# Local attention: one row of heads over all jobs, ordered by a table of times

## The chip, the cores and the metric

One core of one Trainium2 chip runs the whole program. The metric is the device time of one execution in microseconds (us). The kernel before was run three times: 4954.37, 4963.61 and 4968.31 us, median 4963.61 us. One more execution was profiled: 4963.8 us, its span on the engines 4961.9 us.

The five engines run separate instruction streams, each strictly in its own order, and meet at semaphores: PE (TensorE, matrix products and transposes into the accumulator banks), DVE (VectorE), ACT (ScalarE), POOL (GpSimd) and SP (SyncE, which issues all the DMA transfers here).

## The reference, cut to what matters

A residual stream `x` of 4 batch entries x 256 tokens x 256 features passes six stages: cross attention, convolved attention, a local transformer, cross attention, gated linear attention and a mixture of experts. Only the third stage is touched. It computes, six times (layers):

```python
x = attn_layer(shift_tokens(x), Wqkv[i], q_scale[i], k_scale[i], Wo[i]) + x
x = ffn_layer(shift_tokens(x), ln_g[i], ln_b[i], W1[i], b1[i], W2[i], b2[i]) + x
```

`shift_tokens` takes the second half of the features from the token before. `attn_layer` has 16 heads of 64; queries and keys are normalised per head, scaled and rotated, and each token attends to itself and the 64 before it, with a softmax. `ffn_layer` is a layer norm, a product to 2 x 682 columns, GELU gating and a product back to 256. All is float32. Batch entries do not mix, so layer l of entry b needs only layer l-1 of entry b.

## The kernel before, in words

The stage is the class `Local`. Its unit is a job, one layer of one batch entry: 24 jobs, j = 4 l + b. A job has three parts:

- front: `features` (PE transposes 256 tokens of x and of the shifted rows `xs`, ACT copies them to `xt`); eight `proj` (a 128x512 product for tile 0/1, query/key, half 0/1; DVE multiplies it in three instructions with the rotation tables, ACT squares it, POOL adds the two rotated parts); `sumsq` and `norm` (DVE sums the squares; POOL raises them to the power -1/2, L1577); `scale_k` (DVE scales the keys by their norms); eight `turn` (PE transposes queries or keys, ACT copies them out: two instructions for queries, one for keys); four `values` (product on PE, copy on ACT).
- back: the 16 heads of attention, class `Attention`. A head n passes PE `front` (mask, L965, and scores, L967), DVE maximum and scale, ACT exponential (L1036), then `divide` on DVE and POOL (L1023), PE `turn` of the weights (L976), ACT copy (L1043), and for every second head PE `apply` (weights times values, L987) and an ACT copy into `ot` (L1474). `steps` lays this out: head n's front goes with head n-1's divide and head n-3's turn. Called per job, it ends each job with four steps that have no front. Then two `wo`, the output product (L1853).
- gated: `fs` (three DMAs fetch the rows of x and the shifted rows into `fs`, and cannot start before both `wo` results are added to x), `f_stats`, `f_scale`, `ft` (layer norm and its transposes), six `w1` (L1869) with three `gate` (ACT GELU and a DVE product per chunk; GELU and exponential need different tables on ACT, ACT_TABLE_LOAD), two `w2` (L1879), whose results DVE adds to x.

The DMA step `shift` fetches the shifted rows `xs` for the same batch entry of the next layer: one DMA of 127 partitions (L1538) and one of a single row (L1539). It waits on SP for the end of that entry's second `w2`. `fs` has the same pair of DMAs (L1549, L1550) behind one of all 128 partitions (L1548).

`order()` writes one list, `plan`, and every engine walks that list and does its share of each step. So the list fixes the order on each engine, and all timing follows from the order and the waits. Round n of `order()` runs front of job n, back of job n-1 and gated of job n-2; `even` deals their steps out over 24 ticks.

Products and transposes outside attention share three accumulator banks (5, 6, 7) in turn: use number n takes bank 5 + n % 3 and PE waits until use n-3 has been taken out (`freed`). Scores have two banks: head n's front waits for the exponentials of head n-2. Head 0 of a job waits until all eight `turn` results of its job are copied out. `values` of job j overwrites the values of job j-2, so ACT waits for those `apply` steps (`pv_done`, L1628).

Of the kernel before, what the change touches and what calls it, by code (L numbers as in the profile page):

```python
# [1297 lines left out]
class Local(Stage):  # L1298
# [4 lines left out]
    scale = None  # L1303

# [49 lines left out]
    def order(self):  # L1354
# [13 lines left out]
        for n in range(len(jobs) + 2):  # L1368
            parts = [(part(*jobs[n - lag]), steps, late) for lag, (part, steps, late) in
                     enumerate(((self.front, 24, 0), (self.back, 23, 0), (self.gated, 17, 0.1)))  # L1370
                     if 0 <= n - lag < len(jobs)]
            even(*parts)

    def front(self, l, b):
        put = self.plan.append
        if b == 2 and l + 1 < DEPTH:
            put(("load_front", l + 1))
        if b == 3 and l + 1 < DEPTH:
            put(("tables", l + 1))
        yield ()  # L1380

        def project(tile, sec):
            for half in range(2):
                put(("proj", l, b, tile, sec, half))
                yield ()
                put(("sumsq", l, b, tile, sec, half))
            put(("norm", l, b, tile, sec))

        def turn(tile, sec):
            for half in range(2):  # L1390
                put(("turn", l, b, tile, sec, half))
                yield ()

        def values(tile):
            for half in range(2):
                put(("values", l, b, tile, half))
                yield ()
        yield from project(0, 0)
        yield from round_robin(project(0, 1), values(0))
        yield from turn(0, 0)  # L1400
        put(("scale_k", l, b, 0))
        yield from round_robin(project(1, 0), turn(0, 1))
        yield from project(1, 1)
        yield from round_robin(turn(1, 0), values(1))
        if b == B - 1 and l + 1 < DEPTH:
            put(("load_values", l + 1))
        put(("scale_k", l, b, 1))
        yield ()
        if (l, b) != (DEPTH - 1, B - 1):
            l2, b2 = divmod(self.job(l, b) + 1, B)  # L1410
            put(("features", l2, b2))
            if l2 == 0 and b2 + 2 < B:
                put(("shift", 0, b2 + 2))
        yield from turn(1, 1)

    def back(self, l, b):
        put, j = self.plan.append, self.job(l, b)
        for steps in self.at.steps(H * j, [(j, h) for h in range(H)]):
            for s in steps:
                put(("attend", s))  # L1420
# [1177 lines left out]
```

## Time and profile before

| what | value |
|---|---|
| median of three runs | 4963.61 us (4954.37 to 4968.31) |
| profiled execution: time, span | 4963.8 us, 4961.9 us |
| busy PE, DVE, ACT, POOL over the span | 4427.0, 3249.4, 2896.0, 1872.0 us |
| first and last `features` copy of the stage (L1603) | 1361.3 and 3053.7 us after the span's start |
| mean granted PE clock over the span | 0.967 |

The stage runs from about 1360 to 3227 us. "Busy" of PE is modelled: its records overlap, so the length of a PE step is best read from one start to the next. A bracket at the end of a timeline row is the idle time of the engine before it and what ended it; "issue" means that the profile shows nothing that it waited for.

### The profile page before, as it was taken

The page shows a single profiled execution, that of the slowest core. Times are in us where ns is not written, and L with a number is a line of the kernel's source. Part 1 is how long each engine was busy: PE and PEld are TensorE (multiplying, and loading weights), DVE is VectorE, ACT ScalarE, POOL GpSimd, SP SyncE. Part 2 cuts the span into 40 slices and gives each one's busy share as a digit, 9 for nine tenths or more (in the row PEclk, how much of TensorE's full clock was granted, in tenths as well). Part 3 has the DMA queues.
Part 4 walks back from the last instruction along what each step waited for, and adds up shares of the span by engine and source line. Part 5 has one row for each costly group of instructions (what it writes and reads, how often), then busy time and mean ns, then how long its engine had stood idle before and what let it go on. Part 6 is the DMA issues. An engine that isn't in the chain of part 4 may idle for free. (4 is left out here: it accounts for less than half of the span.)

```text
span 4961.9 us, 85570 instructions
## 1 busy us (share of the span) xinstructions
PE 4427.0 (89%) x31624; PEld 3025.6 (61%) x31624; DVE 3249.4 (65%) x7542; ACT 2896.0 (58%) x5798; POOL 1872.0 (38%) x1876
## 2 busy tenths in 40 slices
PE   5899998989789999999999999859999999669999
PEld 3555555547556666666676666635555555358888
DVE  5677777767565666656656666356777777575555
ACT  2666666668556666666666666426666666523332
POOL 2223222215564545445545444223222222035554
PEclk8999999989899999999999999979999999879999
DMA  5655555500110010100001000056555555011110
GB/s 138 131 103 104 104 113 102 94 24 1 56 39 6 23 45 13 54 15 26 33 14 53 16 32 6 13 126 129 108 103 104 110 109 90 12 53 49 49 48 19
DMA packets 189931, 305.60 MB, mean 62 GB/s; under 512 B 19736, under 2 KB 109752, under 8 KB 187832
## 3 DMA queue, kind: packets, MB, share of 16 engines
q1 hardware_dynamic: 189520, 300.13, 27.3%
q8 instruction: 256, 4.19, 0.4%
q14 instruction: 155, 1.27, 0.1%
HBM read 215.81 MB, written 73.40 MB: 58 GB/s over the span
## 5 line engine op out<-in xcount | busy, mean ns | idle before, releaser
L707 DVE TENSOR_REDUCE xa_m_part<-xa_ring 128x1 f32<-128x512 f32 x2048 | 1319.1, 686 | 506.3 <-PE xa_ring L856 491.0
L633 ACT ACTIVATE xa_ex<-xa_sc 128x1024 f32<-128x1024 f32 x1024 | 991.6, 1022 | 114.2 <-PE xa_sc L844 99.0
L856 PE MATMUL xa_ring<-xa_ks,xa_q_base 48*128 48x512 f32 x2048 | 517.8, 498 | 185.6 <-DVE xa_m_part L707 129.4
L870 PE MATMUL xa_pv<-xa_ex,xa_vs 128*17 128x256 f32 x8192 | 547.8, 385 | 1.3 <-issue 1.3
L856 PEld LDWEIGHTS xa_ring<-xa_ks,xa_q_base 48*128 48x128 f32 x2048 | 201.4, 185 | 517.2 <-DVE xa_m_part L707 432.9
L1036 ACT ACTIVATE lt_p<-lt_bank,lt_stat,lt_rq 128x128 f32<-128x128 f32 (+1 forms) x768 | 365.6, 482 | 215.4 <-DVE lt_stat L1006 210.1
L1570 POOL TENSOR_TENSOR lt_r_qk<-lt_r_qk,lt_t_rot 128x512 f32<-128x512 f32 x192 | 243.2, 1267 | 611.1 <-DVE lt_t_rot L1686 606.1
L844 PE MATMUL xa_sc<-xa_q_base,xa_ks 50*128 50x256 f32 x4096 | 423.0, 302 | 26.4 <-ACT xa_k L605 5.2
L844 PEld LDWEIGHTS xa_sc<-xa_q_base,xa_ks 50*128 50x128 f32 x4096 | 346.8, 187 | 117.5 <-ACT xa_vs L620 24.1
L1023 POOL TENSOR_SCALAR lt_p<-lt_p,lt_stat 128x192 f32<-128x192 f32 x384 | 335.0, 876 | 197.8 <-DVE lt_stat L1013 197.8
L2412 PE MATMUL moe_bank<-moe_xp,moe_wp 128*128 128x512 f32 x1536 | 373.3, 392 | 5.9 <-POOL moe_wp L2240 4.2
L1809 PE MATMUL lt_bank<-lt_wqk,lt_xt 128*128 128x512 f32 x768 | 365.5, 599 | 0.7 <-ACT lt_xt L1603 0.7
L555 POOL CAST xa_kp<-xa_k 128x512 fp32r<-128x512 f32 (+1 forms) x144 | 84.4, 586 | 655.7 <-ACT xa_k L613 314.2
L1577 POOL TENSOR_TENSOR lt_nrm<-lt_nrm,minus_half 128x16 f32<-128x16 f32 x96 | 280.5, 2922 | 122.4 <-DVE lt_nrm L1703 121.2
L2412 PEld LDWEIGHTS moe_bank<-moe_xp,moe_wp 128*128 128x128 f32 x1536 | 281.5, 189 | 59.9 <-issue 4.3
L870 PEld LDWEIGHTS xa_pv<-xa_ex,xa_vs 128*17 128x17 f32 x8192 | 188.7, 97 | 198.6 <-issue 59.6
L2275 ACT ACTIVATE moe_sg<-moe_bank 128x512 f32<-128x512 f32 x128 | 76.5, 598 | 341.1 <-PE moe_bank L2412 341.1
L1610 ACT ACTIVATE lt_t_sq<-lt_bank 128x512 f32<-128x512 f32 x192 | 114.6, 597 | 267.3 <-DVE lt_t_rot L1686 267.3
L1869 PE MATMUL lt_bank<-lt_ft,lt_w 128*128 128x256 f32 x1152 | 262.5, 381 | 1.2 <-DVE lt_ft L1751 1.2
L2246 POOL TENSOR_TENSOR moe_hp<-moe_hh,moe_hp 128x512 fp32r<-128x512 f32 x128 | 166.1, 1297 | 256.7 <-ACT moe_hp L2253 256.7
L976 PE MATMUL lt_bank<-ident,lt_p 128*128 128x128 f32 x1152 | 199.3, 282 | 54.7 <-issue 54.7
L1002 DVE TENSOR_REDUCE lt_stat<-lt_bank 128x1 f32<-128x128 f32 (+1 forms) x768 | 210.5, 315 | 44.2 <-PE lt_bank L967 44.0
(281 smaller groups left out, 8755.1 us busy)
## 6 DMA issues: line engine op xcount, KB each, us to landing
xa_ks<-keys SPq DMA_DIRECT2D x384, 256.0 KB, 9.1
keys<-xa_kp SPq DMA_DIRECT2D x128, 512.0 KB, 3.8
xa_cx<-in_ctx_t SPq DMA_DIRECT2D x64, 512.0 KB, 4.9
lt_wqk<-in_lt_wqkv SPq DMA_DIRECT2D x6, 2048.0 KB, 8.4
lt_w<-in_lt_w SPq DMA_DIRECT2D x6, 1536.0 KB, 6.2
xa_q_base<-xa_m_rows SPq DMA_DIRECT2D x512, 2.0 KB
moe_w<-in_moe_wg SPq DMA_DIRECT2D x64, 128.0 KB, 2.2
moe_w<-in_moe_wu SPq DMA_DIRECT2D x64, 128.0 KB, 2.3
```

What stands on the lines that cost most here:

```text
L633: act.activation(x.ex[:, n % x.NE, :, :], x.sc[n % 2][:, :, :], ACT.Exp).then_inc(*x.ex_done.one())
L707: dve.tensor_reduce(x.m_part[:, i % 2, qt, h, ch:ch + 1], x.bank(n + odd), AX.X, ALU.max).then_inc(*x.dve_out.one())
L844: mm = pe.matmul(x.sc[n % 2][:, 2 * odd + pair, :], x.ks[unit % x.NU][rows, 2 * (g % 2) + pair, kt * P:(kt + 1) * P], x.q_base[rows, 2 * g ...
L856: pe.matmul(x.bank(n + odd), x.q_base[rows, pair, b * S + qt * P:b * S + (qt + 1) * P], x.ks[unit % x.NU][rows, pair % 4, ch * 512:(ch + 1 ...
L870: mm = pe.matmul(x.pv[32 * j:32 * j + x.VW, :], x.vs[:, i % x.NV, kt, 4 * g + j, :], x.ex[:, n % x.NE, 2 * (j % 2) + j // 2, :], start=(kt ...
L1023: pool.tensor_scalar(sv, sv, self.stat[:, n % 5, 3, 1:2], None, ALU.mult).then_inc(*self.div_pool.one())
L1036: act.activation(self.p[:, n % 5, to], s[:, at], ACT.Exp, bias=t3[:, 1, q:q + 1], scale=st.scale_of(b, h, slice(q, q + 1)) if st.scale is ...
L1570: pool.tensor_tensor(out, out, self.t_rot[:, t, :], ALU.add).then_inc(*self.rot_add.one())
L1577: pool.tensor_tensor(n[:, 2, :], n[:, 1, :], c.minus_half[:, 0:H], ALU.pow).then_inc(*self.rnorm.one())
L1809: mm = pe.matmul(bank[:, :], self.xt[:, par, k, tile * P:(tile + 1) * P], self.wqk[:, l % 2, k, col:col + 512], start=(k == 0), stop=(k == ...
L1869: mm = pe.matmul(bank[:, gate * S:(gate + 1) * S], self.w1[:, k, gate * FFP + m * P:gate * FFP + (m + 1) * P], self.ft[:, k, :], start=(k ...
L2412: mm = pe.matmul(self.banks[2 * (n % 2) + j][:, :], self.wp[:, wpart, i, j, k * FI:(k + 1) * FI], self.xp[:, xpart, k, at], start=(m == 0) ...
```

## The change: what it does

`order()` no longer runs rounds. Every step of a job has a fixed time, in ticks, from a table; job j adds 24 j; all steps are sorted by time. The heads of all 24 jobs form one row: one call of `steps` over 384 heads, head i at 24.14 + 1.5 i ticks, so the steps without a front come only once, at the very end. Loads, `features` and `shift` have times of their own. The set of steps is the same. In a job's own ticks: first projection at -3.79, last `turn` of keys at 22.93, heads from 24.14 on, `wo` at 56.11 and 56.30, `fs` at 56.72 and `f_stats` at 64.74, `w1` from 69.70 to 74.85, `w2` at 77.48 and 83.33, `shift` at 82.7; `features` of the next job at 15.17. Since job j+1's features come at 15.17 of job j, the job four on, which needs the shifted rows, has its features at 87.17. The order of the head also asks for the change at L1628: half 0 of `values` waits only for the first 8 heads of job j-2, half 1 for all 16.

```diff
--- before.py
+++ after.py
@@ -1301,6 +1301,23 @@
 
     HP = H // 2
     scale = None
+    TICKS, HEADS, FEATURES, SHIFT = 24, 24.14, 15.17, 82.7
+    LOADS = ((16.58, "load_front", 2, ()), (22.82, "tables", 2, ()), (10.8, "load_values", 3, ()),
+             (62.88, "load_back", 3, (0,)), (76.94, "load_back", 3, (1,)), (86.28, "load_back", 3, (2,)))
+    TABLE = ((-3.79, "proj", 0, 0, 0), (-2.03, "sumsq", 0, 0, 0), (-0.97, "proj", 0, 0, 1),
+             (2.44, "values", 0, 0), (2.99, "sumsq", 0, 0, 1), (3, "norm", 0, 0), (3.5, "proj", 0, 1, 0),
+             (3.96, "turn", 0, 0, 0), (4.12, "proj", 0, 1, 1), (5.04, "sumsq", 0, 1, 0),
+             (5.38, "turn", 0, 0, 1), (5.61, "sumsq", 0, 1, 1), (6.7, "values", 0, 1), (6.91, "norm", 0, 1),
+             (7.05, "proj", 1, 0, 0), (8.34, "scale_k", 0), (10.18, "proj", 1, 0, 1), (11.1, "turn", 0, 1, 0),
+             (12.82, "turn", 0, 1, 1), (12.82, "sumsq", 1, 0, 0), (13.07, "sumsq", 1, 0, 1),
+             (13.12, "norm", 1, 0), (13.57, "proj", 1, 1, 0), (13.71, "turn", 1, 0, 0),
+             (13.71, "proj", 1, 1, 1), (14.98, "values", 1, 0), (15.57, "sumsq", 1, 1, 0),
+             (15.59, "sumsq", 1, 1, 1), (17.36, "turn", 1, 0, 1), (19.45, "norm", 1, 1),
+             (20.84, "values", 1, 1), (21.54, "scale_k", 1), (21.93, "turn", 1, 1, 0),
+             (22.93, "turn", 1, 1, 1), (56.11, "wo", 0), (56.3, "wo", 1), (56.72, "fs"), (64.74, "f_stats"),
+             (66.43, "f_scale"), (68.92, "ft"), (69.7, "w1", 0), (69.75, "w1", 1), (69.83, "gate", 0),
+             (71.18, "w1", 2), (72.3, "w1", 3), (72.49, "gate", 2), (74.21, "w1", 4), (74.85, "w1", 5),
+             (74.86, "gate", 4), (77.48, "w2", 0), (83.33, "w2", 1))
 
     def __init__(self, c, g):
         super().__init__(c)
@@ -1365,93 +1382,24 @@
         put(("features", 0, 0))
         put(("shift", 0, 2))
         jobs = [(l, b) for l in range(DEPTH) for b in range(B)]
-        for n in range(len(jobs) + 2):
-            parts = [(part(*jobs[n - lag]), steps, late) for lag, (part, steps, late) in
-                     enumerate(((self.front, 24, 0), (self.back, 23, 0), (self.gated, 17, 0.1)))
-                     if 0 <= n - lag < len(jobs)]
-            even(*parts)
-
-    def front(self, l, b):
-        put = self.plan.append
-        if b == 2 and l + 1 < DEPTH:
-            put(("load_front", l + 1))
-        if b == 3 and l + 1 < DEPTH:
-            put(("tables", l + 1))
-        yield ()
-
-        def project(tile, sec):
-            for half in range(2):
-                put(("proj", l, b, tile, sec, half))
-                yield ()
-                put(("sumsq", l, b, tile, sec, half))
-            put(("norm", l, b, tile, sec))
-
-        def turn(tile, sec):
-            for half in range(2):
-                put(("turn", l, b, tile, sec, half))
-                yield ()
-
-        def values(tile):
-            for half in range(2):
-                put(("values", l, b, tile, half))
-                yield ()
-        yield from project(0, 0)
-        yield from round_robin(project(0, 1), values(0))
-        yield from turn(0, 0)
-        put(("scale_k", l, b, 0))
-        yield from round_robin(project(1, 0), turn(0, 1))
-        yield from project(1, 1)
-        yield from round_robin(turn(1, 0), values(1))
-        if b == B - 1 and l + 1 < DEPTH:
-            put(("load_values", l + 1))
-        put(("scale_k", l, b, 1))
-        yield ()
-        if (l, b) != (DEPTH - 1, B - 1):
-            l2, b2 = divmod(self.job(l, b) + 1, B)
-            put(("features", l2, b2))
-            if l2 == 0 and b2 + 2 < B:
-                put(("shift", 0, b2 + 2))
-        yield from turn(1, 1)
-
-    def back(self, l, b):
-        put, j = self.plan.append, self.job(l, b)
-        for steps in self.at.steps(H * j, [(j, h) for h in range(H)]):
-            for s in steps:
-                put(("attend", s))
-            yield ()
-        for tile in range(2):
-            put(("wo", l, b, tile))
-            yield ()
-        if b == B - 1 and l + 1 < DEPTH:
-            put(("load_back", l + 1, 0))
-
-    def gated(self, l, b):
-        put = self.plan.append
-        put(("fs", l, b))
-        yield ()
-        yield ()
-        yield ()
-        put(("f_stats", l, b))
-        yield ()
-        yield ()
-        put(("f_scale", l, b))
-        yield ()
-        put(("ft", l, b))
-        yield ()
-        for mc in range(0, FC, 2):
-            put(("w1", l, b, mc))
-            put(("w1", l, b, mc + 1))
-            put(("gate", l, b, mc))
-            yield ()
-        if b == B - 1 and l + 1 < DEPTH:
-            put(("load_back", l + 1, 1))
-        for tile in range(2):
-            put(("w2", l, b, tile))
-            yield ()
-        if b == B - 1 and l + 1 < DEPTH:
-            put(("load_back", l + 1, 2))
-        if l + 1 < DEPTH:
-            put(("shift", l + 1, b))
+        timed = []
+        for j, (l, b) in enumerate(jobs):
+            for tick, kind, *a in self.TABLE:
+                timed.append((self.TICKS * j + tick, len(timed), (kind, l, b, *a)))
+            if l + 1 < DEPTH:
+                for tick, kind, when, a in self.LOADS:
+                    if b == when:
+                        timed.append((self.TICKS * j + tick, len(timed), (kind, l + 1, *a)))
+                timed.append((self.TICKS * j + self.SHIFT, len(timed), ("shift", l + 1, b)))
+            if j + 1 < len(jobs):
+                l2, b2 = divmod(j + 1, B)
+                timed.append((self.TICKS * j + self.FEATURES, len(timed), ("features", l2, b2)))
+                if l2 == 0 and b2 + 2 < B:
+                    timed.append((self.TICKS * j + self.FEATURES, len(timed), ("shift", 0, b2 + 2)))
+        heads = self.at.steps(0, [(j, h) for j in range(len(jobs)) for h in range(H)])
+        for i, head in enumerate(heads):
+            timed += [(self.HEADS + self.TICKS * i / H, len(timed) + m, ("attend", s)) for m, s in enumerate(head)]
+        self.plan += [step for _, _, step in sorted(timed)]
 
 
 
@@ -1625,7 +1573,7 @@
             elif kind == "values":
                 tile, half = a[2:]
                 on.wait_ge(self.gen_full, self.use[step] + 1)
-                on.wait_ge(self.at.pv_done, H // 2 * (j - 1))
+                on.wait_ge(self.at.pv_done, H // 2 * (j - 2) + H // 4 * (half + 1))
                 act.activation(self.v[:, par, tile, half * 512:(half + 1) * 512], bank[:, :],
                                ACT.Copy).then_inc(*free.one())
             elif kind == "attend":
```

## Rows read from the trace of the kernel before

**Rows 1.** Busy time per stretch: engine busy us (instructions), granted clock, DMA.

```profile
core 0: us, PE busy (x) PEld busy (x) DVE busy (x) ACT busy (x) POOL busy (x), PEclk, DMA share, GB/s
1360.20:1456.70 96.50, 82.00 (x358) 46.30 (x359) 59.88 (x158) 51.76 (x137) 59.43 (x44) 0.92 0.18 64
1456.70:3053.70 1597.00, 1527.43 (x8067) 1075.03 (x8066) 990.85 (x2950) 1035.75 (x2626) 774.54 (x651) 0.99 0.08 26
1532.60:1609.80 77.20, 73.88 (x386) 51.73 (x385) 47.64 (x142) 49.29 (x125) 36.89 (x31) 0.98 0.02 6
1609.80:1685.30 75.50, 72.19 (x386) 50.97 (x385) 47.04 (x140) 49.31 (x125) 36.88 (x31) 1.00 0.06 20
3128.50:3227.00 98.50, 75.61 (x418) 61.11 (x416) 32.46 (x123) 40.53 (x110) 15.13 (x18) 0.91 0.05 17
```

**Rows 2.** Timeline of ACT: start, duration, what, [idle before].

```profile
1609.80 0.60 ACT L1603 ACTIVATE lt_xt<-lt_bank 128x512 f32<-128x512 f32 x1 [0.19 <-PE lt_bank L1801]
...
1685.34 0.60 ACT L1603 ACTIVATE lt_xt<-lt_bank 128x512 f32<-128x512 f32 x1 [0.19 <-PE lt_bank L1801]
```

**Rows 3.** Timeline of PE in that round.

```profile
1613.49 0.60 PE L1821 MATMUL lt_bank<-ident,lt_r_qk 128*128 128x128 f32 x4
1613.93 3.62 PE L1853 MATMUL lt_bank<-lt_wo,lt_ot 128*128 128x256 f32 x16
1617.38 0.30 PE L965 MATMUL lt_bank<-lt_mask,ident_bf 128*128 128x320 bf16 x1
...
1618.07 1.88 PE L1809 MATMUL lt_bank<-lt_wqk,lt_xt 128*128 128x512 f32 x4
1619.79 0.30 PE L965 MATMUL lt_bank<-lt_mask,ident_bf 128*128 128x320 bf16 x1
...
1628.48 1.88 PE L1809 MATMUL lt_bank<-lt_wqk,lt_xt 128*128 128x512 f32 x4
1630.65 0.31 PE L965 MATMUL lt_bank<-lt_mask,ident_bf 128*128 128x320 bf16 x1 [0.29 <-ACT lt_p L1036]
...
1633.16 0.52 PE L976 MATMUL lt_bank<-ident,lt_p 128*128 128x128 f32 x3 [1.65 <-issue]
...
1642.90 0.71 PE L967 MATMUL lt_bank<-lt_kt,lt_q_odd 128*128 128x128 f32 x4
1644.24 0.52 PE L976 MATMUL lt_bank<-ident,lt_p 128*128 128x128 f32 x3 [0.63 <-issue]
...
1669.66 0.65 PE L1821 MATMUL lt_bank<-ident,lt_r_qk 128*128 128x128 f32 x4 [0.16 <-DVE lt_u L1763]
...
1682.72 0.55 PE L976 MATMUL lt_bank<-ident,lt_p 128*128 128x128 f32 x3
1683.85 0.87 PE L987 MATMUL lt_bank<-lt_pt,lt_v 128*64 128x256 f32 x8 [0.58 <-ACT lt_pt L1043]
```

**Rows 4.** Timeline of POOL around the longest of these waits.

```profile
1627.69 2.93 POOL L1577 TENSOR_TENSOR lt_nrm<-lt_nrm,minus_half 128x16 f32<-128x16 f32 x1 [0.34 <-DVE lt_nrm L1703]
...
1632.29 1.50 POOL L1023 TENSOR_SCALAR lt_p<-lt_p,lt_stat 128x192 f32<-128x192 f32 x2
```

**Rows 5.** Groups of the page (section 5): busy, mean ns, idle before.

```profile
L1036 ACT ACTIVATE lt_p<-lt_bank,lt_stat,lt_rq 128x128 f32<-128x128 f32 (+1 forms) x768 | 365.6, 482 | 215.4 <-DVE lt_stat L1006 210.1
...
L1610 ACT ACTIVATE lt_t_sq<-lt_bank 128x512 f32<-128x512 f32 x192 | 114.6, 597 | 267.3 <-DVE lt_t_rot L1686 267.3
```

**Rows 6.** Timelines of ACT and DVE at a gate of the same round.

```profile
1653.55 1.28 ACT L1642 ACT_TABLE_LOAD   x1
1654.85 0.84 ACT L1642 ACTIVATE lt_gl<-lt_bank,lt_ffc 128x256 f32<-128x256 f32 x2
...
1655.35 0.88 DVE L1763 SCALAR_TENSOR_TENSOR lt_u<-lt_bank,lt_ffc,lt_gl 128x256 f32<-128x256 f32 x2 [2.88 <-ACT lt_gl L1642]
```

**Rows 7.** Timelines of SP and DVE: shifted rows requested, issued, waited for.

```profile
1695.14 7.18 SPq L1550 DMA_DIRECT2D lt_fs<-x_sb  x1
...
3192.21 0.69 SPq L1549 DMA_DIRECT2D lt_fs<-x_sb  x1
...
3201.87 0.43 DVE L1731 BATCH_NORM_STATS2 lt_fst<-lt_fs 128x6 f32<-128x256 f32 x1 [10.30 <-DMA lt_fs<-x_sb]
```

## The prediction, made before the changed kernel ran

> **What bounds the kernel now.** I read the page first, then the busy times by stretch, then one round of PE from start to start. Six stages follow one another with a barrier between, and only the third changes, so everything outside about 1360 to 3227 us stays. Inside, PE is busy 1527 of 1597 us between the third features copy and the last, while DVE, ACT and POOL are busy 991, 1036 and 775 us [rows 1]: PE is the bound, and the other engines have a third or more of their time free. The stretch of 1597 us holds 21 rounds. The one that I take as pattern goes from one features copy to the next in 75.54 us [rows 2]; it repeats to the tenth, except that six of the 21 take 77.2 us: in those the granted clock is 0.98 in place of 1.00 [rows 1], a short spell at 1.2 instead of 2.4 GHz that costs 1.7 us. Check: 21 x 75.54 + 6 x 1.7 = 1596.5.
>
> Busy time hides what PE loses, so I went through the round by starts. A turn of queries or keys takes 0.44 us, an output product 3.45, a head's front 0.69, a projection 1.72 [rows 3]. Against these lengths the round has five waits that work of PE does not fill:
> - a projection of 1.72 us occupies 2.17 before the next front can go, since the exponentials of two heads back are not done: 0.45 lost [rows 3];
> - a front at 1630.65 should take 0.69, and the next step comes after 2.51: 1.82 lost. The profile calls it issue; POOL shows why: the power -1/2 takes 2.93 us, and the divides of two heads, which the turn needs, stand behind it until 1632.29 and after [rows 3, 4];
> - the same once more behind the scores at 1642.90: 1.34 for 0.55 (a front's 0.69 less 0.14 of mask), 0.79 lost [rows 3];
> - at the end of the round, where heads 14 and 15 have no front between them any more, 1.13 for 0.33, 0.80 lost, to ACT's copy of the weights [rows 3];
> - a turn that waits for the bank of a gated product, a bracket of 0.16 and 0.38 in all with what precedes it [rows 3].
> Together 4.24 us. The rest, 75.54 - 4.24 = 71.30 us, is what PE's work of one job takes with no wait at all. This is the number on which the forecast stands: a new order cannot make a round shorter than 71.3 us, and all it can give is 21 x 4.24 = 89 us, the six slow spells (10 us), and something at the two ends.
>
> **The change part by part.** Instructions are the same in kind and number; nothing is added on any engine, and ACT switches tables six times per job as before, as every gate still stands between exponentials. So the sum is made of waits alone.
>
> *Waits that go.* Heads come every 1.5 ticks (71.3 x 1.5 / 24 = 4.5 us) where they came every 3.3 us (head 0's front stands 49 us of PE work before head 15's) with an end of four steps without fronts. The exponentials of two heads back then have 9 us for a chain of about 2.5 us on DVE and ACT, the end without fronts is gone, and between each norm and the turn that needs a divide behind it I count at least 3.5 us of POOL's slack in the new list (tightest: the norm of tile 1's queries, with the divide of head 8 behind it and that head's turn 9.7 us of PE work later, against 5.4 on POOL: 4.60 from the power's start to the first divide behind it, and 0.8 for that divide [rows 4]). All of 0.45 + 1.82 + 0.79 + 0.80 goes: 3.86 us, and the 0.38 changes its place.
>
> *Waits that come.* I wrote out one period of the new list (job 8's fronts, head 11 of job 6 to head 10 of job 7, gated of job 5), added PE's lengths along it, and put beside every bank, score bank and table the time at which ACT, DVE and POOL are done, in their own order. ACT takes 0.60 us to copy or square a bank, 0.48 for each of a head's two exponentials, with the reads behind them taken as 1.3 [rows 5], 1.28 for a table, which starts right behind ACT's last instruction and not at the gate's turn, then 0.84 for two GELUs [rows 6]. Six places come out late:
> - head 0 waits for the last turn of its job, which stands on ACT behind a gate, a table and head 15: 0.5;
> - the query turn behind projection (0,1,1) waits for the bank of the projection three uses back: 0.4;
> - the first w2 waits for a query turn's two copies (1.2) behind head 2's exponentials: 0.7;
> - the projection behind the last gate: 0.1; head 13's front, as f_stats delays head 11 on DVE: 0.3; the first w1, which needs the ft copy on DVE: 0.5.
> Sum 2.5 us, so a round of 73.8. Bounds: 0 if each of these is covered, 5 if ACT is one instruction later at each. I take 2.5. The gain is 75.54 - 73.8 = 1.75 per round, 21 x 1.75 = 37 us.
>
> *The slow spells.* They come only in rounds that hold the 1.82 us wait. In the new list no wait is over 0.7, so I count them gone: 10 us, with 0 and 15 as bounds (15 if the short spells outside go too).
>
> *The relaxed wait of `values`.* It is what lets half 0 stand before the last applies of job j-2. In the new list half 0 comes behind heads 8 to 11's apply and half 1 behind the last; neither waits. Worth 0 by itself; without it ACT would wait there.
>
> *fs and f_stats.* fs is asked for right behind wo and used 18 us later; shifted rows need 9.7 us from the second request (3192.21 to 3201.87) [rows 7]. Covered; before it was too, in a steady round.
>
> *Shifted rows of the next layer.* Before, `shift` had a quarter of a round and more before the features; now it starts when the second w2 is added, and from there to the features the list leaves PE 11.0 us of work (three fronts, two applies, three turns of weights, two turns, two projections, one values). The chain is two additions on DVE 0.85, handing over 0.1, rows 9.66: 10.6 us. Spare: 0.4 us. Cost taken 0; see the first rival.
>
> The row shows 127 KB on their way for 9.7 us, and no row shows two such requests at once. The Trainium skill, page "DMA: Bandwidth & Descriptors", section "Why a DMA increments its semaphore by 16 and not by 1", says that a transfer over 127 partitions is put on a single DMA engine, where 128 would use sixteen. By that rule the rows of fs and of shift queue on one engine, and shift would be about 1 us later here than alone: 0.6 us per round, 12 us in all and 4927 us, against nothing and 4915 by the row alone.
>
> *Ends.* First two jobs: 96.5 us, with 82.0 busy and clock 0.92 [rows 1]. The new list puts four more PE steps ahead of the second tile's key turn, and job 1's first projections before job 0's last turns; the two waits for norm and scale_k shrink by some 4 us. Bounds -8 and +4; taken -2. Last stretch: 98.5 us with 75.6 busy [rows 1]; its heads are closer together than ACT can take them, as before, and the one new thing is the second w2 of job 22 in the 14 us hole of the last fs: -2.6. On the other side heads 6 to 13 have less between them: +2.6. Taken 0, bounds -6 and +6.
>
> Sum: 37 + 10 + 2 = 49 us. Against the profiled execution's 4963.8 us (0.2 above the median) this gives 4915 us.
>
> **The rivals.**
> *First: features wait for the shifted rows.* For it: the spare of 0.4 us is less than a handful of handings-over, fs asks only some 8 us earlier for the same kind of rows that take 9.7, and the issue of the single row behind them once took 7.18 us, beside a load [rows 7]; loads of the next layer stand behind `shift` in two of four rounds. Against: those loads are asked for after the rows. Price: 0.6 to 3.0 us per round in the 20 rounds that use shifted rows of a layer before; at 1.2 it is 24 us, so 4939 us.
> *Second: none of the six waits is real*, since ACT and DVE run ahead where I have them late; rounds of 71.8 us give 21 x 3.7 + 10 + 2 = 90 us: 4874 us. Against it: ACT's and DVE's own order before also showed 0.45 and 0.38 us waits at such places.
> *Third, slower: the job's edge on ACT.* Head 0 can go only after gate, turn, table, head 15, weights copy and last turn: 0.84 + 0.6 + 1.28 + 1.3 + 0.5 + 0.6 = 5.1 us on ACT [rows 5, 6], against 5.3 us of PE work from the second w1 to head 0. DVE does the gate's products (0.88 [rows 6]), a sum of squares and head 15's maximum in between, 2.9 us or so. If these add to ACT's chain instead of overlapping it, the wait at head 0 is 0.5 + 2.9 = 3.4, and after a wait of that length the slow spell (1.7) may fall in every round: 71.3 + 2.0 + 3.4 + 1.7 = 78.4 against a mean of 1597 / 21 = 76.05 before, 21 x 2.35 = 50 us more, 5014 us. It decides from 4.7 us of new waits and spells per round on. Against it: DVE's share runs while ACT loads its table [rows 6].
>
> **How the numbers follow.** Forecast 0.58, first rival 0.2, second 0.12, third 0.1. The likeliest gives 4915 us. Its own range is 4895 to 4935. Outside it I go down to 4880, which takes in most of the second rival's side, and up to 4952, past the first rival's middle and its dear end of 3.0 us per round only in part. A difference under 0.3%, 15 us, is what a measurement of this kernel can tell from none: the border is 4949 and 4978. Faster: forecast, second, and most of the first: 0.85. Same: the dear end of the first and a mild third: 0.07. Slower 0.08.
>
> **What would show it.** Features copies 73.8 us apart in the middle, where they were 75.5, to be read first. No POOL power in front of a late turn of weights; the brackets on L976 from issue gone. PE's waits on L965 at head 0, on L1879 and on L1869, half a microsecond each. No features waiting for a DMA: a bracket there on L1801 would be the first rival. Granted clock 1.00 through the middle. The forecast is wrong if a round is over 75 us or under 72.5, or if the stage's ends move by more than 10 us.

## The result: 2.4% faster, and a round without a single wait

The kernel after takes 4843.88 us (median of four runs, 4835.19 to 4853.14), the kernel before 4965.24 beside it: ratio 0.9764, interval 0.975 to 0.9777. The forecast was 4915 us with a range from 4880 to 4952: the direction is right, but the time lies outside the range, and the gain is two and a half times what I worked out (121 for 49 us). The profiled execution takes 4844.9 us, its span 4843.0; the granted clock over the span is as before, 0.966 for 0.967. All stages outside the local one together are as long as before within 0.5 us: of 118.9 us less in the span, 118.4 lie between the first and the last matmul of the local stage, 1866.4 us before and 1748.0 after.

Busy times by stretch come first, as in [rows 1]: from the start to the fourth features, twenty rounds, the end of the stage, and then a single round. A round is the time from one features copy to the next.

```profile
core 0: us, PE busy (x) PEld busy (x) DVE busy (x) ACT busy (x) POOL busy (x), PEclk, DMA share, GB/s
1361.10:1493.20 132.10, 122.84 (x576) 74.67 (x577) 91.92 (x250) 77.59 (x213) 88.20 (x67) 0.96 0.14 49
1493.20:2918.80 1425.60, 1424.62 (x7679) 1026.86 (x7677) 904.67 (x2811) 974.57 (x2501) 747.31 (x620) 1.00 0.09 29
2918.80:3109.50 190.70, 173.91 (x966) 134.65 (x963) 91.38 (x311) 105.50 (x279) 61.82 (x57) 0.96 0.03 11
1565.40:1636.60 71.20, 71.20 (x386) 51.32 (x385) 44.99 (x140) 48.69 (x126) 37.30 (x31) 1.00 0.07 21
```

In the middle PE is busy 1424.62 of 1425.60 us. The same 386 matmuls that took 75.5 us [rows 1] take 71.20, with PE idle for 0.0, and DVE, ACT and POOL run as many instructions in it as before (140, 126 and 31, for 140, 125 and 31). The granted clock is 1.00 throughout: the six spells in which PE ran at 1.2 instead of 2.4 GHz are gone. Features copies stand 71.24 us apart nineteen times (72.0 in the first of the twenty rounds); before it was 75.5 us fourteen times, 75.9 once and 77.2 six times.

The groups of the profile's page answer [rows 5]: the means are the old ones (480 ns for 482; POOL's power 2929 for 2922 on the page of the kernel before), so nothing runs faster; only the order differs.

```profile
L1036 ACT ACTIVATE lt_p<-lt_bank,lt_stat,lt_rq 128x128 f32<-128x128 f32 (+1 forms) x768 | 365.5, 480 | 344.7 <-DVE lt_stat L1006 338.9
...
L1525 POOL TENSOR_TENSOR lt_nrm<-lt_nrm,minus_half 128x16 f32<-128x16 f32 x96 | 281.2, 2929 | 128.1 <-DVE lt_nrm L1651 128.0
```

ACT's idle time before the exponentials rose from 215.4 to 344.7 us. This costs nothing: ACT waits more now, mostly for DVE's scaled maximum, and PE no longer waits.

Where the 118.4 us went. I took every step of PE's list (a front, an apply, a projection and so on) from its start to the next start, and subtracted what that step takes where nothing holds it. A check without steps: 24 rounds of 71.24 us are 1709.8, which leaves 156.6 us of the stage before and 38.2 of the stage after; the table has 156.8 and 38.4.

| part of the stage | PE's waits before | after | change | forecast |
|---|---|---|---|---|
| the rounds, with the slow spells | 100.9 us | 1.1 us | -99.8 | -47 |
| both ends | 55.9 us | 37.3 us | -18.6 | -2 |

The next view is the job's edge, the place of my third rival and of one of the dearer new waits of the forecast: timelines of ACT, DVE and PE around head 0's front in the kernel after, with rows left out where three dots stand.

```profile
1649.73 0.84 ACT L1590 ACTIVATE lt_gl<-lt_bank,lt_ffc 128x256 f32<-128x256 f32 x2 [0.61 <-PE lt_bank L1817]
1650.24 0.88 DVE L1711 SCALAR_TENSOR_TENSOR lt_u<-lt_bank,lt_ffc,lt_gl 128x256 f32<-128x256 f32 x2 [2.62 <-ACT lt_gl L1590]
1650.46 0.60 ACT L1572 ACTIVATE lt_kt<-lt_bank 128x512 f32<-128x512 f32 x1
1651.08 1.28 ACT L1036 ACT_TABLE_LOAD   x1
...
1652.40 0.46 ACT L1036 ACTIVATE lt_p<-lt_bank,lt_stat,lt_rq 128x128 f32<-128x128 f32 x1
1652.75 0.19 ACT L1036 ACTIVATION_READ_ACCUMULATOR lt_p<-lt_bank,lt_stat,lt_rq 128x1 f32 x1
1652.85 0.50 ACT L1036 ACTIVATE lt_p<-lt_bank,lt_stat,lt_rq 128x192 f32<-128x192 f32 x1
1653.34 0.48 ACT L1043 ACTIVATE lt_pt<-lt_bank 128x384 f32<-128x384 f32 x1
1653.71 0.60 ACT L1572 ACTIVATE lt_kt<-lt_bank 128x512 f32<-128x512 f32 x1
...
1654.86 0.30 PE L965 MATMUL lt_bank<-lt_mask,ident_bf 128*128 128x320 bf16 x1
```

Read the starts, not the durations. The last turn's copy ends at 1653.71 + 0.60 = 1654.31, and head 0's front, which needs it, starts at 1654.86 without a bracket: 0.55 us to spare, where I had 0.5 us of waiting. A head's exponentials with their reads occupy ACT from 1652.40 to 1653.34, which is 0.94 us; I had put them in at 1.3. The copy of the weights has a record of 0.48, and the next instruction starts 0.37 after it. Of the 1.05 us between my reckoning and the chip, this one head explains 0.36 + 0.11, and the two GELUs 0.11 more: the kt copy starts 0.73 after them, and their record says 0.84. The remaining half microsecond is not accounted for here.

### The profile page after: what moved, and what is told of

It is laid out like the page before. It is cut to its first block and busy times, and to the rows that moved or that the text cites. A ratio compares the mean times of both kernels' runs of the same rounds, so it can differ in the third digit from the quotient of the medians.

```text
span 4843.0 us, 85571 instructions
## 1 busy us (share of the span) xinstructions
PE 4401.1 (91%) x31624; PEld 3032.8 (63%) x31624; DVE 3206.5 (66%) x7542; ACT 2877.7 (59%) x5794; POOL 1884.3 (39%) x1876
## 5 line engine op out<-in xcount | busy, mean ns | idle before, releaser
L1036 ACT ACTIVATE lt_p<-lt_bank,lt_stat,lt_rq 128x128 f32<-128x128 f32 (+1 forms) x768 | 365.5, 480 | 344.7 <-DVE lt_stat L1006 338.9
L1023 POOL TENSOR_SCALAR lt_p<-lt_p,lt_stat 128x192 f32<-128x192 f32 x384 | 346.6, 903 | 541.6 <-DVE lt_stat L1013 539.0
L1525 POOL TENSOR_TENSOR lt_nrm<-lt_nrm,minus_half 128x16 f32<-128x16 f32 x96 | 281.2, 2929 | 128.1 <-DVE lt_nrm L1651 128.0
L1002 DVE TENSOR_REDUCE lt_stat<-lt_bank 128x1 f32<-128x128 f32 (+1 forms) x768 | 209.1, 313 | 56.1 <-PE lt_bank L967 54.0
L1630 DVE TENSOR_TENSOR lt_r_qk<-lt_bank,lt_tab 128x512 f32<-128x512 f32 x192 | 132.7, 691 | 168.3 <-PE lt_bank L1757 167.3
L1817 PEld LDWEIGHTS lt_bank<-lt_ft,lt_w 128*128 128x128 f32 x1152 | 214.8, 192 | 46.1 <-issue 21.6
```

What stands on the lines that cost most here:

```text
L1023: pool.tensor_scalar(sv, sv, self.stat[:, n % 5, 3, 1:2], None, ALU.mult).then_inc(*self.div_pool.one())
L1036: act.activation(self.p[:, n % 5, to], s[:, at], ACT.Exp, bias=t3[:, 1, q:q + 1], scale=st.scale_of(b, h, slice(q, q + 1)) if st.scale is ...
L1525: pool.tensor_tensor(n[:, 2, :], n[:, 1, :], c.minus_half[:, 0:H], ALU.pow).then_inc(*self.rnorm.one())
L1817: mm = pe.matmul(bank[:, gate * S:(gate + 1) * S], self.w1[:, k, gate * FFP + m * P:gate * FFP + (m + 1) * P], self.ft[:, k, :], start=(k ...
```

## Experiments

Eleven kernels ran besides the change. The kernel before took 4962.71, 4957.21 and 4957.84 us in the three sets (7, 7 and 19 runs); ratios are against it.

### Does POOL's power explain the old round?

```
-  pool.tensor_tensor(n[:, 2, :], n[:, 1, :], c.minus_half[:, 0:H], ALU.pow)
+  pool.tensor_scalar(n[:, 2, :], n[:, 1, :], 0.01, None, ALU.mult)
```

> The kernel before, with POOL's power -1/2 of the norms (2.9 us each, 96 of them) replaced by a multiplication by a constant: the norms, and so the output, are not the reference's. Theory POOL: the 1.82 and the 0.79 us in which PE waited for a turn of weights are the divides of heads behind this power, and the short spells of half clock follow the longer of the two. Then both go in all 24 jobs and the six spells too: 24 x 2.6 + 10 = 72 us less, rounds of 72.9 us, about 4892 us. Rival: PE waits there for ACT or DVE and the power only happens to run at the same time; then under 20 us, 4945 us or more.

It leaves out the power, so the norms are not the reference's. 4930.63 us, ratio 0.9933 (0.9912 to 0.9954); rounds of 75.0 us. That is 32 us, between the 72 of the theory and the 20 of the rival, and a quarter of the difference to the kernel after, not most of it. The timeline of PE over a round, its longest waits:

```profile
1519.34 0.87 PE L987 MATMUL lt_bank<-lt_pt,lt_v 128*64 128x256 f32 x8 [0.58 <-ACT lt_pt L1043]
...
1542.40 0.31 PE L965 MATMUL lt_bank<-lt_mask,ident_bf 128*128 128x320 bf16 x1 [1.00 <-ACT lt_p L1036]
```

So the power did cause the 1.82 and the 0.79 us: no turn of weights waits any more, and the slow spells are gone. But a front now waits a full microsecond for the exponentials, 0.29 before [rows 3], and a plain round is only 0.6 us shorter for 2.6 us of waits removed. In the old order, most of what one wait gives up comes back at others.

### One row of heads alone, the table alone

row_old_steps keeps the row and gives the other work in even steps, nearly in the old order (the values of tile 0 come after the first turns):

```
-  for tick, kind, *a in self.TABLE: ...
+  for part, steps, first, width in ((self.front, 24, 0, 24), (self.gated, 17, 57.2, 21.6)): ...
+  wo at ticks 54.6 and 55.6
```

> One row of heads over all jobs, every 1.5 ticks, as in the changed kernel, but front and gated steps evenly spaced one after the other as the old generators gave them (gated 6.8 ticks later, values of tile 0 after the first turns), no table. Theory ROW: what the change brings comes from the heads lying 4.5 us apart with no end per job; a coarse even order round them does as well: rounds of 71.3 to 72.5 us, 4845 to 4875 us. Rival TABLE: the fine placing of the 54 steps is what hides ACT, DVE and POOL; then rounds keep 2 us or more of waits: 4895 us or more.

5119.74 us, ratio 1.0312 (1.0293 to 1.033): slower than before, with rounds of 82.6 us, about every third of 84. The theory ROW is refuted: a coarse even order round the row does not do. Its PE timeline, the two longest waits:

```profile
1635.88 5.38 PE L1875 MATMUL lt_bank<-lt_wo,lt_ot 128*128 128x256 f32 x16 [3.08 <-ACT lt_ot L1496]
...
1658.50 1.06 PE L1843 MATMUL lt_bank<-ident,lt_r_qk 128*128 128x128 f32 x8 [2.94 <-DVE lt_r_qk L1734]
```

table_heads_per_job keeps the table and gives each job its own heads:

```
-  heads = self.at.steps(0, [(j, h) for j in range(len(jobs)) for h in range(H)])
+  for j: heads of job j alone, head i at HEADS + 24 * (j + i / 20)
-  (56.11, "wo", 0), (56.3, "wo", 1), (56.72, "fs")
+  (52.6, "wo", 0), (52.8, "wo", 1), (53.2, "fs")
```

> The table of the changed kernel, but the heads laid out job by job as before: 1.2 ticks (3.6 us) apart and four steps without fronts at each job's end; wo and fs 3.5 ticks earlier. Theory ROW: the waits of closely packed heads come back, 0.8 us at the end of each job and 0.5 to 1.8 on scores or divides: rounds of 73 to 75, 4885 to 4930 us. Rival TABLE: the placing alone is enough, rounds of 71.3 and 4845 us.

5037.24 us, ratio 1.0148 (1.013 to 1.0165); rounds of about 80 us. Both its theories missed. As placed here, row and table are worth nothing apart: each is 70 to 160 us slower than before, and together they are 120 faster. That does not price either at its best, as each was set beside an order that it was not fitted to.

row_spaced asks what the table adds to the row. It is row_old_steps with the distances widened at three places:

```
   wo 54.6 / 55.6 -> 56.2 / 57.2, gated work from 58.2
   scale_k: four steps ahead of the first turn of keys (was: directly ahead)
   f_scale: three steps ahead of ft (was: one)
```

> One row of heads over all jobs as in the kernel after, but the other work of a job once more in even steps, in the order of the kernel before. Beside row_old_steps (rounds of 82.6 us, 5119.74 us) only distances are changed: the output projection 1.6 ticks later and so two ticks behind the apply of heads 14/15, the key scaling four steps ahead of the first turn of keys, three steps instead of one between the scaling of the shifted features and their transposition. Theory (what the table gives is the distance, in TensorE's own work, between a producer on ACT, DVE or POOL and the matmuls that need it): the waits of 3.23, 1.76, 3.10 and 1.38 us in a round of row_old_steps go, 9.5 us, and what is left is 73 to 75 us a round, 4900 to 4950 in all, close to before. Rival (the row needs the table's order, which mixes the parts of a job in another way; distance at these four places only moves the waits on to the next step): rounds of 78 us or more, over 5000 us.

4953.12 us, ratio 0.999 (0.998 to 0.9999), 167 us less than row_old_steps; most rounds 75.4 to 75.6, four of 77.3 to 77.6. Both lie just above what the theory gave (73 to 75 us, up to 4950), and far from the rival's 78 and 5000. PE's idle time before the output products, the turns and the transposes of the shifted features, in the window 1500:2900, fell from 52.3, 49.5 and 21.0 to 0.0, 2.8 and 0.0 us. A part moved one step on: before w1 it rose from 9.3 to 41.9, and its largest wait is for the layer-normed features.

```profile
2567.11 3.69 PE L1894 MATMUL lt_bank<-lt_ft,lt_w 128*128 128x256 f32 x16 [1.66 <-DVE lt_ft L1776]
```

So at these places what counts is the amount of PE's own work between a producer on another engine and the matmul that needs it. The 4.2 us a round between this kernel and the kernel after were not taken apart further.

### How fine is the fit of row and table?

```
-  TICKS, HEADS, FEATURES, SHIFT = 24, 24.14, 15.17, 82.7
+  TICKS, HEADS, FEATURES, SHIFT = 24, 24.64, 15.17, 82.7
```

> The kernel after with its whole row of heads half a tick (1.5 us of TensorE work) later against the table. Theory (a round without a wait has small margins that I read from its trace: 0.55 us at head 0 behind the job's edge, 0.4 us between the row of heads and some turns; the table is fitted to one alignment): the output projection comes 1.5 us nearer to the last apply, and waits of 0.5 to 2 us a round appear, rounds 71.7 to 73.2 us, 4855 to 4890. Rival (the distances are wide and the alignment of row and table is free): rounds stay at 71.2, 4840 to 4848 us.

4954.75 us, ratio 0.9994 (0.9982 to 1.0006): half a tick costs the whole gain. Both theories missed; mine had the right sign, but the rounds are 76.6 to 77.3 us, at least 5.4 more, where I expected up to 2. Groups of PE instructions between 1600 and 2900 us, idle time before them last:

```profile
L1757 PE MATMUL lt_bank<-lt_wqk,lt_xt 128*128 128x512 f32 x539 | 255.2, 596 | 23.4 <-DVE lt_u L1711 23.4
...
L1827 PE MATMUL lt_bank<-lt_w,lt_u 128*128 128x256 f32 x408 | 95.4, 383 | 9.9 <-ACT lt_q_odd L1569 9.9
L1769 PE MATMUL lt_bank<-ident,lt_r_qk 128*128 128x128 f32 x540 | 82.0, 274 | 22.2 <-DVE lt_u L1711 22.2
...
L1749 PE MATMUL lt_bank<-ident,x_sb 128*128 128x128 f32 x34 | 7.0, 286 | 21.1 <-issue 21.1
```

In the kernel after all four have 0.0 there. The last group is the features waiting for the shifted rows: they start 0.09 us after the rows' last semaphore update, in round after round. The first and the third end at the gate's product, and the timelines of ACT and PE at one show how half a tick becomes 1.46 us.

```profile
2510.61 0.46 ACT L1036 ACTIVATE lt_p<-lt_bank,lt_stat,lt_rq 128x128 f32<-128x128 f32 x1
...
2512.18 0.47 ACT L1036 ACTIVATE lt_p<-lt_bank,lt_stat,lt_rq 128x128 f32<-128x128 f32 x1
...
2514.12 1.28 ACT L1590 ACT_TABLE_LOAD   x1
2515.42 0.84 ACT L1590 ACTIVATE lt_gl<-lt_bank,lt_ffc 128x256 f32<-128x256 f32 x2
...
2516.46 1.98 PE L1757 MATMUL lt_bank<-lt_wqk,lt_xt 128*128 128x512 f32 x4 [1.46 <-DVE lt_u L1711]
```

The gate stands behind the exponentials of two heads and the table; in the kernel after one head alone stands between this gate and the one before it. PE needs the bank that the gate's product gives back, and gets it 1.46 us late.

### Is an engine full, or were my starts late?

```
+  for m in range(3 if tile and half else 0):
+      act.activation(self.more, src[:, 0:2, :], ACT.Copy)      # ahead of the last turn's copy
```

> The changed kernel with three more ACT copies of 128x256 (0.38 us each, one after the other, some 1.3 us) in front of the last turn's copy, for which head 0 of the job waits. Theory STARTS: ACT's instructions follow each other closer than their durations say (a head's exponentials 0.94 us from start to start where the durations add to 1.35), the chain had 0.55 us to spare and I had counted it 0.5 late; then 0.7 to 0.9 us of waiting per round, 17 to 20 us more, 4862 us. Rival: ACT has several us to spare here: 4844 us. Rival SUM OF DURATIONS: no spare, 1.3 us per round, 30 us more, 4874 us.

4858.15 us, ratio 0.9803 (0.9788 to 0.9818). The added copies hold ACT from 1658.51 to 1659.62, 1.11 us, and PE waits for head 0, in the timelines of ACT and PE:

```profile
1658.51 1.22 ACT L1576 ACTIVATE lt_more<-lt_bank 128x256 f32<-128x256 f32 x3
1659.62 0.59 ACT L1578 ACTIVATE lt_kt<-lt_bank 128x512 f32<-128x512 f32 x1
...
1660.27 0.31 PE L965 MATMUL lt_bank<-lt_mask,ident_bf 128*128 128x320 bf16 x1 [0.45 <-ACT lt_kt L1578]
```

w1 starts at 1657.92 and needs 1.73 us; the front starts at 1660.27, so 0.62 is lost. The rounds are 71.86 us, 0.62 longer. 1.11 us of work added, 0.62 of it seen: a spare of 0.5, as the starts gave (0.55), where by durations all 1.11 would have come on top of 0.5 of waiting.

```
+  pool.tensor_tensor(self.more[:, pn % 2, :], n[:, 1, :], c.minus_half[:, 0:H], ALU.pow)
```

> The changed kernel with POOL's power -1/2 done twice (2.9 us more per norm, 96 norms, to a tile that nobody reads). Theory SLACK: between each norm and the first turn of weights behind it on POOL there are 4 us or more of slack, and so are there to scale_k; rounds stay at 71.2 to 71.8: 4846 to 4860 us. Rival: the order only just covers one power; then 1.5 to 2.9 us at each of two or more norms per round, 4 us x 24: 4930 us or more.

4864.27 us, ratio 0.9811 (0.979 to 0.9833), 20 us more than the kernel after, all of it at the ends and nearly all at the start. Rounds stay at 71.2 with every power on POOL done twice:

```profile
1500.00:2860.00 1360.00, 1358.46 (x7324) 979.62 (x7323) 847.65 (x2685) 929.24 (x2389) 926.39 (x669) 1.00 0.09 29
```

In the first jobs features stand 36.8, 56.1, 58.0 and 73.8 us apart for 30.8, 43.2, 57.2 and 72.0. In the middle a norm has at least the 2.9 us of one more power to spare; where a job starts without heads of another beside it the power is on the path.

### The shifted rows

```
-  (83.33, "w2", 1)
+  (84.5, "w2", 1)
```

> The changed kernel with the second w2 of each job 1.17 ticks later, behind the front, apply and turn of heads that stood after it; features stay. So the shifted rows of the next layer are asked for 2.0 us later against the features that need them (20 jobs). Theory ROWS NEAR: from the request to the features there were 10.1 us in the changed kernel, and rows take about 9.4 to 9.7, so 1.3 to 1.6 us of waiting per round: rounds of 72.7, and 26 to 32 us more, about 4872 us. Rival ROWS FAR: they have 3 us or more to spare, nothing moves: 4844 us.

4871.44 us, ratio 0.9835 (0.9819 to 0.9852); rounds of 72.5 to 72.9, as expected. PE's timeline at the features:

```profile
1636.89 0.41 PE L1749 MATMUL lt_bank<-ident,x_sb 128*128 128x128 f32 x2 [1.11 <-issue]
```

The request stood at 1627.72, so the rows were there 9.2 us after it. In the kernel after, features start 9.86 us after the request (1625.52 to 1635.38) and do not wait. The semaphore's last update comes 9.1 to 9.4 us after the request there, which leaves 0.5 to 0.8 us to spare. Here the request comes 1.8 us later against the features, and 1.1 to 1.4 of that is seen as waiting.

The same 127 rows, cut into 112 and 15 partitions, for the features and for fs:

```
-  sp.dma_start(xs[1:P, :, :], y[0:P - 1, ...])
+  for lo, hi in ((1, 113), (113, P)):
+      sp.dma_start(xs[lo:hi, :, :], y[lo - 1:hi - 1, ...])
```

> The changed kernel with each copy of 127 partitions cut in two, 112 and 15 partitions. Theory ONE ENGINE: 127 rows run on one DMA engine and take 8.4 us, 112 and 15 rows are spread and take 2 to 4 us. In the middle that is hidden; at the last job the 14 us between wo and the layer norm's transposes fall by 5 to 6, and the rows' spare before features rises from about 1.7 to 6 us or more. Time: 4838 us. Rival: the 512-byte rows are slow whichever engine takes them, nothing moves: 4844 us. Neither theory has rounds below 71.2 us.

4822.81 us, ratio 0.9716 (0.9699 to 0.9732). The expectation was 4838. Counted from the request to the last update of their semaphore, the rows of the rounds are in place after 9.1 to 9.4 us in the kernel after and after 3.3 to 4.6 cut, and the spare before the features grows from 0.5 to 0.8 us to 5.3 to 6.6. (The 8.4 and 1.7 us in the expectation are not borne out: 8.4 fits a landing counted from the second request of the pair, and the spare a distance counted from the first.) The cost on SP is not in the request of 127 partitions, which takes 0.7 us, but in the single row's behind it. SP's timeline in one round of the kernel after, then with the rows cut:

```profile
1696.76 0.71 SPq L1486 DMA_DIRECT2D lt_xs<-x_sb  x1
1697.82 4.26 SPq L1487 DMA_DIRECT2D lt_xs<-x_sb  x1
```

```profile
1682.64 1.59 SPq L1487 DMA_DIRECT2D lt_xs<-x_sb  x2
1684.27 0.57 SPq L1489 DMA_DIRECT2D lt_xs<-x_sb  x1
```

The rounds had nothing to gain, and the gain lies at the stage's two ends. At its start PE waits for the mask, whose transfer SP issues behind two such pairs. From the last matmul of the stage before to the first of this one it is 31.55 us in the kernel after and 21.08 with the rows cut (10.5 us less). At its end the hole of the last fs is 6.3 us shorter. That is 17 us of the 24 between the two profiled executions; the other 7 lie in the stages outside, which this change does not touch. PE's timelines at the start of the stage and at the last job, in the kernel after:

```profile
1361.13 0.66 PE L1749 MATMUL lt_bank<-ident,x_sb 128*128 128x128 f32 x2 [31.55 <-DVE lt_p L1604]
...
3087.43 1.08 PE L1808 MATMUL lt_bank<-ident,lt_fs 128*128 128x128 f32 x4 [11.33 <-DVE lt_fs L1688]
```

The same with the rows cut:

```profile
1346.95 0.66 PE L1753 MATMUL lt_bank<-ident,x_sb 128*128 128x128 f32 x2 [21.08 <-DVE lt_p L1608]
...
3067.01 1.08 PE L1812 MATMUL lt_bank<-ident,lt_fs 128*128 128x128 f32 x4 [5.03 <-DVE lt_fs L1692]
```

In the packet records of one round (job 8) the 254 packets of 512 bytes of these rows start one behind another over 7.0 us; cut, all 254 start within 1.1 us. The prediction cites the Trainium skill, page "DMA: Bandwidth & Descriptors", section "Why a DMA increments its semaphore by 16 and not by 1": a transfer over 127 partitions runs on a single DMA engine. This trace agrees in that the packets come one behind another and that cutting off the remainder makes the landing about 2.8 times as fast (9.1 us to 3.3). Which engine carried them the trace does not show.

Both edits in one kernel:

> The same later second w2, with the copies of 127 partitions cut into 112 and 15. ROWS NEAR: if the wait of the kernel beside it is for the rows, it is gone here, as the cut rows land some 6 us earlier: rounds of 71.2 us, 4823 us. If the later w2 costs by its place in the bank order and not by the rows, rounds stay at what the other kernel shows.

4825.78 us, ratio 0.9742 (0.9722 to 0.9762), rounds of 71.2: the late w2 costs nothing in the rounds once the rows are quick. The wait in a_late_w2 is the rows'.

### A version that beats both

a_split_rows, with the mask's transfer first in the stage, and the last job but one's two w2 steps behind the last job's request for rows:

```
+  put(("load_mask",))                                   # now ahead of load_front
+  late = {("w2", 0): 80.8, ("w2", 1): 81.2}             # job 22;  f_stats of job 23 at 57.0
```

> The kernel after with a_split_rows (the copies of 127 shifted rows cut into 112 and 15) and two edits at the stage's ends: the band mask is the first transfer of the stage, and the two w2 steps of the last job but one stand behind the last job's output projection and its requests for shifted rows, with the last job's feature statistics between them on VectorE. Theory: at the stage's start TensorE waited until 1346.95 for VectorE's copy of the mask, behind SP's eight requests issued from 1338.9 on: 4 to 7 us less. At its end the hole before the last job's transposition (5.03 us with one w2 step in it) takes the other one, 2.75 us: 2.3 to 2.75 less. Rounds stay at 71.2. Together 7 to 9 us under a_split_rows (4822.8), so 4814 to 4816. Rival for the first edit (TensorE waits for the first layer's weights, not for the mask, as the weights are requested next): 0 there, and 4820.

4822.18 us, ratio 0.9729 (0.9711 to 0.9746): faster than before and after, and no different from a_split_rows. The second edit did what it should (the hole is 2.43 us, was 5.03), but the stage as a whole is only 1.8 us shorter. The first is refuted: the mask is ready early, but PE's first matmul comes 21.83 us after the last of the stage before (21.08 in a_split_rows), now held by the transfer of the rows and not, as the rival had it, by the weights.

```profile
1346.28 0.66 PE L1756 MATMUL lt_bank<-ident,x_sb 128*128 128x128 f32 x2 [21.83 <-DMA lt_xs<-x_sb]
```

## Why the prediction was wrong

- *PE bounds the stage; its bare work is 71.30 us a round.* Right, to 0.1 us: 71.24. The five waits were real, and their sum of 4.24 is within 0.1 of the 4.3 us by which a plain round shrank.
- *Waits that go, 3.86.* Right: all of it went, and the 0.38 I let change its place went too.
- *Waits that come, 2.5.* **This term failed.** None of the six exists in the rounds; 2.5 x 21 = 53 us of the 71 that were missing. I added record durations along ACT's and DVE's lists, while records of neighbours overlap there: 0.94 us from start to start for what I counted as 1.3, 0.73 for 0.84. I had read PE by starts and the other engines by durations. At three places the rows show how far off the reckoning was: head 0 has 0.55 us to spare where I had a wait of 0.5, the first w2 0.33 where I had 0.7, and the first w1 0.76 where I had 0.5. For head 0 the rows above give half of the error to the overlap of records, and a_act_twice confirms the spare. That the same overlap made the other five waits is argued, not tested. The rows of ACT, PE and DVE at w2 and at w1:

```profile
1671.09 0.60 ACT L1569 ACTIVATE lt_q_odd<-lt_bank 64x512 f32<-64x512 f32 x1
1672.02 2.75 PE L1827 MATMUL lt_bank<-lt_w,lt_u 128*128 128x256 f32 x12
...
1644.31 1.00 DVE L1699 TENSOR_SCALAR lt_ft<-lt_bank,lt_lnc 128x256 f32<-128x256 f32 x2 [0.80 <-PE lt_bank L1808]
1646.07 3.19 PE L1817 MATMUL lt_bank<-lt_ft,lt_w 128*128 128x256 f32 x14
```

- *Bounds of that term.* I gave 0 to 5 and chose the middle, though five of the six terms were 0.5 us or less, within the error of the method. The second rival, which said that none of the six is real, was given 0.12. So the kernel did what the second rival said. Its own price was still high: rounds of 71.8 for 71.24 are 12 us, and the ends 17: 4874 - 12 - 17 = 4845, the measured execution.
- *Slow spells, 10 us.* Right: the granted clock is 1.00 from 1493 to 2919, and six times 1.7 us went. That they went in b_cheap_norm as well fits their coming with the wait behind the power. It doesn't show what sets them off: a_heads_later has a wait of 1.46 us in its rounds and no spell.
- *Ends, -2.* **This term failed too**, by 17 us. I worked them out from the first two jobs' norms and the last fs only, and took the rest as evened out. The brackets of PE from the last features copy on add up to 26.1 us before and 16.8 after. The hole of the last fs gave 2.7 of that, as forecast, but the old tail also had waits of 1.24, 0.66, 0.47 and 2.23 us between its close heads and once more the waits behind a norm (1.66 and 0.63). All of these went, where I had put +2.6 for the heads. Up to the third features copy the brackets fell from 14.5 to 7.7 us. a_double_norm shows how much of the start hangs on POOL: some 20 us for one more power per norm.
- *Shifted rows: spare 0.4, no cost.* Right: a spare of 0.5 to 0.8 us, since the rows land 9.1 to 9.4 us after the request and not after 9.66. The first rival was near: a request 1.8 us later brought waits of 1.1 to 1.4 in a_late_w2, and half a tick brought them in a_heads_later. The microsecond that two transfers on one engine would have added, by the rule of the Trainium skill that the prediction cites, does not show: alone, in the kernel before, the rows took 9.1 to 9.5 us in most rounds.
- *Third rival, ACT at the job's edge.* Not here: 0.55 us to spare. That the order is that finely fitted was no empty fear: in a_heads_later half a tick puts four waits into a round and takes back everything. But they stand at the banks behind the gates, at w2 and at the features, not at head 0.

The prediction named its own signs of being wrong: a round under 72.5 us, or ends that move by more than 10. Both came.

## What to carry to other kernels

Walk the order of every engine by start-to-start distances taken from a place where that engine runs without a gap; added record durations overstated the chain at head 0, and a forecast made of half-microsecond waits so found is within its own error. When one engine bounds a stage, bound the worth of a new order by that engine's bare work, and count the ends with the same list of waits. Of the five orders tried here one reached the bare work, two came out where they began and two were worse. What an order must supply is enough of the bound engine's own work between every producer and its consumer, for all pairs at once; half a tick of misfit cost as much as the old order.

## What the runs showed of the hardware

- A copy of 127 partitions x 1 KB within SBUF with a single row's copy behind it: in place 9.1 to 9.4 us after the first request, with SP held for 5.3 to 5.6 us, 4.3 to 4.7 of it by the single row's request. With the 127 cut into 112 + 15: in place after 3.3 us in most rounds, 4.6 at most, and SP held for 2.2 (kernel after and a_split_rows, rounds).
- A table load on ACT starts 0.02 us behind the previous instruction and does not wait for its activation's input: in the kernel after one runs from 1647.84 to 1649.12, and the GELU behind it waits for PE until 1649.73.

```profile
1647.84 1.28 ACT L1590 ACT_TABLE_LOAD   x1
1649.73 0.84 ACT L1590 ACTIVATE lt_gl<-lt_bank,lt_ffc 128x256 f32<-128x256 f32 x2 [0.61 <-PE lt_bank L1817]
```

- Three ACT copies of 128x256 have a record of 1.22 us together and hold the engine 1.11 (a_act_twice).
- POOL's power on 128x16 takes 2.93 us; the multiplication in its place in b_cheap_norm takes 0.25.
